# Two small sums of the second layernorm's statistics moved from VectorE to ScalarE, and a fence on the w2 loads replaced, in a causal attention plus BitLinear-FFN layer on eight cores

## What is computed

```python
x = layernorm(x + attention(x))          # causal, 16 heads of 64, E = 1024, S = 4096, B = 4
h = layernorm(x)                          # ln1
h = bitlinear(h, w1, b1)                  # activations rounded to 127 steps a row, weights to -1/0/1; 1024 -> 4096
h = gelu(h)
h = layernorm(h)                          # ln2, over 4096
out = layernorm(x + bitlinear(h, w2, b2)) # 4096 -> 1024
```

## Time and profile before

| | |
|---|---|
| time, median of two runs | 2730.37 us |
| the profiled execution's own time | 2740.65 us |
| its span on the slowest core (core 0) | 2739.1 us |
| spans of the eight cores | 2681.3 to 2739.1 us |
| TensorE busy | 1790.8 us (65%) |
| ScalarE busy | 1382.8 us (50%) |
| VectorE busy | 951.0 us (35%) |
| GpSimd busy | 255.1 us (9%) |
| stage 4, from the first FFN matmuls to the end | about 1802 to 2739 us |

### The profile page before, as it was taken

The page is one execution under the profiler, slowest core; times in us unless marked ns, Lnnn a source line. Parts: engine busy times, 40 slices in busy tenths (PEclk is TensorE's granted clock), DMA queues, the critical chain, the costliest instruction groups (busy, mean ns, idle before and its releaser), DMA issues.

```text
span 2739.1 us, 31470 instructions; the slowest of 8 cores (2681.3 to 2739.1 us)
## 1 busy us (share of the span) xinstructions
PE 1790.8 (65%) x9312; PEld 689.5 (25%) x9412; DVE 951.0 (35%) x2196; ACT 1382.8 (50%) x2603; POOL 255.1 (9%) x454
## 2 busy tenths in 40 slices
PE   2999966888757777687585222256676576755766
PEld 1444432222221122222222111222222222322222
DVE  0111110000130111311424656336557564575644
ACT  0222215888739887177162222365646456464553
POOL 1000010000000000000000001203121131311303
PEclk9887768899975788788776555579897898987979
DMA  9122031000055310100101426425143351533415
GB/s 139 18 30 32 0 59 34 1 1 1 1 168 186 123 62 1 47 1 1 47 1 57 144 92 211 105 53 169 67 157 100 108 169 50 173 100 108 145 56 177
DMA packets 63004, 218.69 MB, mean 80 GB/s; under 512 B 12660, under 2 KB 12660, under 8 KB 60533
## 3 DMA queue, kind: packets, MB, share of 16 engines
q0 software_dynamic: 43040, 132.68, 18.5%
q1 hardware_dynamic: 16918, 67.21, 7.1%
q10 hardware_dynamic: 2880, 16.78, 1.7%
HBM read 227.64 MB, written 14.68 MB: 88 GB/s over the span
## 4 chain that ended last, share of the span: by engine, by line
PE 44%; DVE 15%; ACT 15%; issue 15%; DMA 9%; POOL 1%; DVEq 1%; ACTq 0%; SPq 0%; POOLq 0%
PE ps L464 10%; PE ps L1278 9%; ACT ptb L608 5%; PE ps L627 5%; PE ps L586 5%; PE ps L639 3%; PE ps L677 3%; ACT ptb L605 2%; PE ps L1530 2%; DVE cvx L1426 2%; DMA kvx<-w2spill 2%; DVE ternb L933 2%; DMA wstA<-w 2%; PE ps L563 2%; DMA onesfb<-onesf 2%
## 5 line engine op out<-in xcount | busy, mean ns | idle before, releaser
L605 ACT ACTIVATE ptb<-ps 128x512 bf16<-128x512 f32 (+7 forms) x640 | 338.4, 529 | 139.8 <-PE ps L643 110.4
L608 ACT ACTIVATE ptb<-ps 128x512 bf16<-128x512 f32 (+7 forms) x640 | 336.1, 525 | 0.0
L586 PE MATMUL ps<-QT,kvx 64*128 64x512 bf16 (+7 forms) x640 | 248.9, 389 | 127.1 <-ACT ptb L608 111.9
L464 PE MATMUL ps<-xT,qkvw_sb 128*128 128x512 bf16 x996 | 278.0, 438 | 9.9 <-DVE xT L454 7.1
L627 PE MATMUL ps<-ptb,onescb 128*64 128x512 bf16 (+7 forms) x640 | 261.9, 409 | 21.0 <-DVE ptb L619 10.8
L639 PE MATMUL ps<-ptb,kvx 128*64 128x512 bf16 (+7 forms) x640 | 255.4, 399 | 25.7 <-DVE attnT L663 25.7
L1530 PE MATMUL ps<-kvx,q2t 128*128 128x512 bf16 x739 | 209.5, 412 | 91.3 <-DMA kvx<-w2spill 46.8
L1278 PE MATMUL ps<-kvx,q1t 128*128 128x512 bf16 x1007 | 261.3, 403 | 10.8 <-DVE q1t L1265 6.6
L631 PE MATMUL ps<-ptb,onescb 128*64 128x512 bf16 (+7 forms) x640 | 268.1, 419 | 0.0
L616 DVE TENSOR_TENSOR ptb<-ptb,dmaskb 128x64 bf16<-128x64 bf16 x256 | 49.3, 193 | 598.4 <-ACT ptb L608 596.6
L643 PE MATMUL ps<-ptb,kvx 128*64 128x512 bf16 (+7 forms) x640 | 256.5, 401 | 0.0
(11 more groups left out here) (166 smaller groups left out, 2795.9 us busy)
## 6 DMA issues: line engine op xcount, KB each, us to landing
kvx<-w2spill POOLq DMA_DIRECT2D x256, 256.0 KB, 4.2
wsbuf<-w2spill POOLq DMA_DIRECT2D x128, 256.0 KB, 3.9
wstA<-w SPq DMA_DIRECT2D x32, 512.0 KB, 5.3
wstA<-w SPq DMA_DIRECT2D x8, 2048.0 KB, 7.8
xkvbf<-xkv POOLq DMA_DIRECT2D x8, 1024.0 KB, 10.3
xres<-xq SPq DMA_DIRECT2D x16, 512.0 KB, 3.4
wbuf<-w ACTq DMA_DIRECT2D x16, 512.0 KB, 3.5
wbuf<-w SPq DMA_DIRECT2D x16, 512.0 KB, 3.3
```

Of the source, the lines that this page charges most:

```text
L464: r = eng.matmul(ps[bk][:, 0:512], qkvw_sb[:, ec * 3 * E + typ * E + p * 128: ec * 3 * E + typ * E + (p + 1) * 128], xT1[:, ec * 512:(ec + ...
L586: eng.matmul(ps[sA][:, noff:512], kt_ap(kb, p, 0, 64), QT[0:64, p * 512 + noff:(p + 1) * 512], start=True, stop=True, tile_position=(0, 0))
L605: eng.activation(ptb[:, ptA + noff: ptA + 512], ps[sA][:, noff:512], AF.Exp, bias=cSH, scale=c0125)
L608: return eng.activation(ptb[:, ptB + noff: ptB + 512], ps[sB][:, noff:512], AF.Exp, bias=cSH, scale=c0125)
```

## The change

Three edits. `f2s`, a VectorE sum over four values, becomes a ScalarE ACTIVATE (Identity) over the four values whose accumulator is the sum; its plain output goes to four unused columns of `lnst`, which is why it also names the resource `lnb1`. `f2q`, a VectorE addition, becomes a ScalarE ACTIVATE with one summand as input and the other as bias. And a load of a streamed chunk depends on the write of that chunk to `w2spill` instead of on `spfence` (the memset stays in the program).

```diff
             def f2s(eng, gco=gco, dstc=dstc):
-                return eng.reduce_sum(cvals[:, dstc:dstc + 1],
-                                      cvx[:, gco - 2:gco + 2], AX.X)
-            sd.step("vector", f2s,
+                return eng.activation(lnst[:, 16:20], cvx[:, gco - 2:gco + 2],
+                                      AF.Identity, bias=f32(0.0),
+                                      scale=f32(1.0),
+                                      accum_out=cvals[:, dstc:dstc + 1])
+            sd.step("scalar", f2s,
                     reads=[f"gco{gco - 2 + nn}" for nn in range(4)] +
-                          [f"cv{dstc}"],
-                    writes=[f"cv{dstc}"], name=f"f{ti}2s{hf}")
+                          [f"cv{dstc}", "lnb1"],
+                    writes=[f"cv{dstc}", "lnb1"], name=f"f{ti}2s{hf}")
             dstq = Q + 9 + hf
             def f2q(eng, dstq=dstq, dstq2=dstq2):
-                return eng.tensor_add(cvals[:, dstq:dstq + 1],
+                return eng.activation(cvals[:, dstq:dstq + 1],
                                       cvx[:, dstq2 - 1:dstq2],
-                                      cvx[:, dstq2:dstq2 + 1])
-            sd.step("vector", f2q,
+                                      AF.Identity,
+                                      bias=cvx[:, dstq2:dstq2 + 1],
+                                      scale=f32(1.0))
+            sd.step("scalar", f2q,
...
-                reads=[f"wst{ssl2}", "spfence"], writes=[f"wst{ssl2}"],
+                reads=[f"wst{ssl2}", f"wsp{cc2}"], writes=[f"wst{ssl2}"],
```

## The result

The changed kernel took 2741.73 us in the median of 35 runs (2718.43 to 2780.81); the kernel before, run beside it, 2720.74 us (34 runs, 2691.03 to 2772.83). The ratio is 1.0059 with a 95% interval of 1.0036 to 1.0083: about 16 us slower, 10 to 23, and well inside the 2% that count as no change. (The medians are over all runs; the ratios leave out those in which the chip was in its slower state, so 2741.73 - 2720.74 = 21 us is not the effect.) A second comparison later gave 1.0023 (0.9978 to 1.0068). An estimate from both, weighted by the widths of their intervals, is 1.0051 (1.0030 to 1.0072): +14 us, 8 to 20. The prediction was 2742 us, +11.3.

The account below looks back on a forecast made before the run. No single engine was taken to bound the kernel, but a chain of TensorE pieces and ScalarE-VectorE relays. Terms 3.2 + 8.1 = 11.3 us on the 2730.4 us median gave 2742 us, 0.4% slower, range 2705 to 2774.

Parts of the forecast that it names:

- The relay of every tile: ScalarE-to-VectorE handover from the last Square to the statistics: 0.2 us longer a tile, 3.2 us over 16 tiles.
- The first copy: VectorE copy moved ahead of a small statistics step (L1382 before) in odd tiles: delays it by 0.43 us.
- The dependent pairs: Odd tile's tail on VectorE: all four L1420 directly behind their own L1414 instead of one, +0.58 us.
- Tile 1: Has another VectorE order, with later statistics but a sooner maximum; counted like other odd tiles at 1.01 us.
- The sum: Relay cost over 16 tiles plus order cost over eight odd tiles: 3.2 + 8.1 = 11.3 us slower.
- Relief of VectorE: Rival: VectorE stops waiting for ScalarE's accumulators and all 10.2 us come back, 2720 us; chance 5%.
- Slower clock: Rival: longer tails make later even tiles start TensorE at the 1.2 GHz level, 32 us more, 2773; chance 7%.
- Table loads: Rival: Identity between gelu and Ln needs another table set, loads of 1.28 us, 2750 us; chance 2%.
- The port rule: Rival: moved VectorE copies lock GpSimd's load issues out of the shared port, 16 us, 2758 us; chance 4%.
- All hidden: Rival: slack in the relay hides all or nearly all of the added delays, 2730 us; chance 14%.
- The signs: Profile signs to check, among them a pair of tiles taking 116.5 us instead of 115.06.

Follow-up runs that it names:

- e1: Kernel before with both half sums moved to ScalarE and the new load fence, VectorE's other instructions in the old order; ratio to before 1.0009.
- e9: The same as e1 but with the old fence: the kernel before with only the two sums moved to ScalarE; ratio to before 1.0013.
- e2: Changed kernel with its new VectorE order kept, but both sums sent back to VectorE directly ahead of the statistics; ratio to before 1.0031.
- e3: Changed kernel with, from tile 3 on, the first copy of odd tiles put back behind the fused subtraction's place; ratio to before 1.0007.
- e4: Changed kernel with, from tile 3 on, the last nine VectorE instructions of odd tiles' tails back in the old order; ratio to before 1.0006.
- e6: Kernel before with only the fence of the streamed loads replaced; ratio to before 0.9978.
- e10: Changed kernel with only tile 1's 13 VectorE steps put back in the old order; ratio to before 1.0011.
- e11: Changed kernel with six more ACTIVATEs with accumulator reads ahead of `f2s`, into unused columns; ratio to before 1.0061.
- e7: Kernel before, orders kept, with the statistics behind the last Square in fewer dependent VectorE instructions; ratio to before 0.9950.

## Why the prediction was right, and where it was off

*The relay of every tile.* Taken: +0.2 us, 3.2 in all. Measured: +0.12 (e1, e9, and even tiles of the changed kernel), 1.9 in all. The interval from the Square's accumulator read to the statistics is 0.48, at the low end of 0.46 to 0.56; the 0.09 for a pointer operand was right (0.29 for `f2q`).

*The first copy.* Taken: +0.43 an odd tile. Measured: 0.44 (e2, and taken back by e3).

*The dependent pairs.* Taken: +0.58. Measured: 0.58 (e2, and taken back by e4). In some tiles the second copy waits for TensorE too, 0.45 us in the one shown, so the mean over the tiles is 0.66; the prediction had this wait only in its bound.

*Tile 1* was counted like the others, at 1.01, since its statistics would come later and its maximum sooner after them. So it is: the pair of tiles 0 and 1 is 2.1 us longer, and tile 1's tail 1.1 us shorter (means of the cores; 8.7 us before, 7.5 and 7.7 in the two traces of the changed kernel). 1.0 remains.

*The sum.* 1.01 us an odd tile and 0.2 a tile were right in the first term (1.02) and a little too large in the second (0.12). In the stretch, which holds 15 relays and seven tails, the measured parts make 9.3 us, and the stretch is longer by 849.4 - 843.2 = 6.2. So the step of the prediction that adds the local delays up at full size was too large by a third here, though all its terms of the order were right. Two traces of each kernel say where the other 3 us are given back (means of the cores; the first line is the measurement itself):

| part of the stretch | the parts make | measured |
|---|---|---|
| tile 0 to tile 1 | +2.1 | +2.1 |
| seven even-to-odd parts (relay 0.12 + 0.44 each) | +3.9 | +2.9 |
| tile 1 to tile 2 (tail -1.1, relay 0.12) | -0.9 | -0.7 |
| the next five odd-to-even parts (tail 0.58, relay 0.12 each) | +3.5 | +3.4 |
| the last odd-to-even part, to tile 14 | +0.7 | -1.5 |
| sum | +9.3 | +6.2 |

The tail and the relay behind it reach the next even tile almost whole. What is given back lies at the last pair above all, and goes with the slow starts: 7 and 8 of the 8 cores begin tile 14 with one in before and e6, 3 and 3 in the changed kernel. The part that leads to tile 14 takes 73.6 us with a slow start and 70.4 without one in the changed kernel (73.3 and 69.5 in before and e6), so nine slow starts fewer on 16 cores are 1.8 us. In the earlier parts it is 71.3 against 67.8 to 68.6: a slow start costs about 3 us. Since e2, e3, e4 and e10 have 6 or 7 slow starts at that place, it is not shown that the changed kernel's fewer ones come from the change; they may be chance.

*The time.* 11.3 us were predicted, and both comparisons together say 14, 8 to 20. That the median of 2741.73 us falls on the predicted 2742 is luck: the kernel of before was 10 us faster in that comparison than in the two runs from which the forecast started, and the difference of the two medians is 21 us. 6.2 us of the difference are in the stretch, and the longer tail of tile 15 behind it would add about 0.6. Where the rest would lie, no trace shows; it may be the scatter of the times.

*The rivals.* Relief of VectorE fell: VectorE is 7 us less busy, and idle for 1801 us of the span where it was 1788; the wait is now at L1367. Slower clock: such starts are real and cost about 3 us each, but a longer tail didn't bring more of them, 4 and 6 instead of 9 and 11. Table loads: 33 on each core before and after. The port rule: the prediction applied it to copies that read PSUM, beside which no issue took over 0.55 us; issues do wait beside L1605, before and after alike. All hidden: e11 refutes the slack in the relay. The signs: a pair of 116.5 us was expected instead of 115.06. The pairs from 2144.68 and 2261.61 take 116.93 and 115.66, and over all cores the median pair from one odd tile's Exp to the next is 116.4, against 115.5 and 115.8 in before and e6. So a pair grew by about 0.8 us and not by 1.4.

## What to carry to other kernels

Where a list scheduler orders the work, an edit that takes instructions off an engine can cost more by the places it gives to others than by itself: compare the order, and look on the critical relay for a bulk instruction that has slipped ahead of a small one (here 0.44 us) and for dependent neighbours that had been apart (0.20 us each). Work taken off an engine that waits gained nothing here; what paid was to shorten the chain of dependent small instructions between two engines, as e7 does (0.57 us a tile, 0.5% of the time). And where times scatter by 0.4%, a stretch between two fixed instructions over all cores tells kernels apart that the times don't, here from about 3 us on. Local delays need not add up over it: 5.4 and 9.2 us for the two halves of the change, 6.2 for the whole.

## What the runs showed of the hardware that was not expected

- Two 128x1024 bf16 `tensor_tensor` instructions on VectorE start 0.80 us apart if the second reads what the first wrote, 0.60 if not; any instruction between them hides it.
- A product of two one-column values as an ACTIVATE with a pointer scale on ScalarE (0.29 us) is slower than the way to VectorE and back: 0.68 against 0.57 us from the Exp to the next ACTIVATE.
- TensorE's slow starts. In the kernel before and e6, 15 of 20 were at the last pair (rows 9 and 10 are one of them: granted clock 0.50, the 1.2 GHz level of the two, behind a load wait of 4.36 us). In e1 and e9, 13 of 28 were there. Whether the sums on ScalarE in the old order give more of them (14 and 14) and the changed kernel fewer (4 and 6; e2 and e10 have 11 each, as e6), or whether this is chance, is open: the waits of TensorE for loads, 5.3 to 5.8 us in the median of the odd-to-even parts in these kernels, are too alike to tell, and no run varied them alone.
- In all 14 traces every load issue of GpSimd that took over 0.62 us instead of 0.54 (25 to 46 a trace, up to 1.07) ran beside a `tensor_scalar` of VectorE on data in SBUF: L1605 in nearly all, L1249 in the others. None grew for a copy from PSUM alone.
